# Attention: queries and keys projected and split once, spread into 64-row blocks by PE with 0/1 products, and the turned maxima added one step later

## The chip, the core and the metric

One core of a Trainium2 chip runs the whole program. The metric is the device time of one execution in microseconds (us). Five engines work side by side, each on its own list of instructions in order: PE (matrix products and 128x128 transposes, which end in PSUM), DVE (vector operations), ACT (element-wise functions), POOL (further element-wise operations and the indirect transfers) and SP (transfers). They are ordered against each other only by counting semaphores: an instruction can wait for a count, and everything behind it on its engine waits with it.

## What is computed

The reference runs a convolution-style block with sampled attention, then an ordinary attention layer, then a mixture of experts over four images of 256 tokens and 128 channels. The change is in the attention layer. Cut to what matters here (`_ln_t` is a layer norm over channels):

```python
q = heads(x @ wq.T)                       # 8 heads of 16 channels
k = heads(x @ wk.T)
v = heads(x @ wv.T)
attn = softmax(einsum('bhnd,bhmd->bhnm', q, k) * 16 ** -0.5)
out = einsum('bhnm,bhmd->bhnd', attn, v)
t = t + out @ wproj.T                     # with x = _ln_t(t)
...
t = t + ffn(_ln_t(t))                     # each token goes to 2 of 16 experts
```

## The kernel before

All of this is one program with its order written out by hand on every engine. After the sampled attention and a feed-forward layer (until 155 us of the profile) comes the attention, then the routing of tokens to experts, and the experts.

**Units and steps.** The attention is cut into 8 units (`UNITS`). Unit u is image b = u // 2 and one half of the heads, g = u % 2, so 4 heads (`UH`). All four engines go through `unit_step(k)` for k = 0 to 9, and in step k do a part of unit k+1 (make queries and keys), k (scores and their row maxima), k-1 (scores the other way round, exponentials) and k-2 (weighted values, division by the sum).

**64-row blocks.** To get products of fp32 accuracy out of the one-pass type fp32r, each query and key is split into a high part (the rounded value) and a low part (the rest). A head has 64 rows (`HROWS`) on the partition axis: for queries 16 rows of the high part, 16 of the low part, 16 of the high part again, and 16 rows for the negated row maximum and zeros; for keys high, high, low, and a row of ones (`one_row`, at row `SPLIT`). One product over the 64 rows then gives the whole score, less its maximum. Two heads lie above each other in 128 partitions.

**How the blocks come about before.** The weights `wq` and `wk` arrive from the host three times over (`thrice`, L1763), so that a projection lands in all of the rows. POOL splits these weights into `wqk_h` and `wqk_l` (L486 to L494). ACT writes the normed tokens twice, as `z1_h` (rounded, L716) and `z1` (L531), and DVE takes the difference `z1_l` (L1019). For each unit and for queries and keys apart, PE's `project(u, of_keys)` (L1460) runs 6 fp32r products of 256 columns into PSUM bank 6 or 7; ACT's `high_parts` (L653) writes the high parts, and DVE's `parts` (L1023) adds the low ones.

**The rest of a step.** `scores(u, pair)` (L1474) is 4 products for two heads; DVE's `row_max` (L1031) reduces each of the 4 heads; PE's `turn_max` (L1489) transposes the 4 maxima into bank 5, and DVE's `max_rows` (L1038) adds them to the queries. `scores_t(u, pair)` (L1500) then gives the transposed scores, ACT's `exp_scores` (L664) takes the exponentials, two at a time, `weigh_values` (L1513) multiplies them with the values, ACT's `unit_out` (L671) copies the result, PE's `turn_out` (L1528) transposes it, and DVE's `unit_norm` (L1045) divides by the sums.

**Waits around it.** PSUM banks 6 and 7 hold one projection each, so a new one waits for the last reader of the old one. Scores of unit k wait for its queries and keys (`qk_ready`), and `scores(k, 1)` for the maxima of `scores(k, 0)` (banks 0 and 1).

**After the loop.** In steps 8 and 9 (`k == UNITS` and the one behind it) the first half of the tokens goes on to its routing: `turn_outputs(0)`, `output_logits(0)`, `project_out(0)`, `rank(0)` on PE; `rank_logits(0)`, `choose(0)`, `residual(0)`, `moments`, `scale(0)` and `place(0)` on DVE. `place(0)` writes the slot numbers (`slots`, L1112), and POOL scatters the tokens with 16 indirect transfers (L514). The second half follows.

Of the kernel before, what the change touches and what calls it, by code (L numbers as in the profile page):

```python
# [55 lines left out]
def columns(**widths):  # L56

    at, where = 0, {}
    for name, n in widths.items():
# [7 lines left out]
                      geglu=2 * GE * P, denseT=GE * P, pout=C, wq=AH * HROWS, wk=AH * HROWS, wv=C, wproj=C, wprojT=C, gate=E)  # L67
# [5 lines left out]
def build(nc, x, weights, vectors, rows, w1_t, w2_t, out):  # L73
    with ExitStack() as ctx:
# [32 lines left out]
        row_groups = sb("row_groups", [P, 2, 4])  # L107
        row_group = sb("row_group", [P, 4])

        raw_by = sb("raw_by", [P, 2])  # L110
        high_by = sb("high_by", [P, 2])
        one_row = sb("one_row", [P, 1])
        sel = sb("sel", [P, 4, NP, P], BF16)
# [106 lines left out]
        with ExitStack() as rounded:  # L220
            xm, wqk_h, wqk_l, z1_h, z1_l = (rounded.enter_context(nc.sbuf_tensor(name, [P, n * T], F32R)) for name, n in (
                ("xm", 4), ("wqk_h", 1), ("wqk_l", 1), ("z1_h", 1), ("z1_l", 1)))
        late = sb("late", [P, 8 * T])
        xm_h, xm_l = (xm[:, 2 * n * T:2 * (n + 1) * T].rearrange("c (s t) -> c s t", s=2) for n in range(2))
# [69 lines left out]
        def sems(names):  # L294
# [27 lines left out]
        geglu_parted, hn_h_ready, hn_l_ready, wqk_parted, z1_h_ready, z1_l_ready = sems(  # L322
            "geglu_parted hn_h_ready hn_l_ready wqk_parted z1_h_ready z1_l_ready")
        gate_mm, lin_mm, gelu_ready, ff_ready, x1_mm, x1_ready = sems(
            "gate_mm lin_mm gelu_ready ff_ready x1_mm x1_ready")
        qk_mm, high_ready, qk_ready, v_mm, v_ready, zeroed = sems(
            "qk_mm high_ready qk_ready v_mm v_ready zeroed")
# [108 lines left out]
        def _(pool):  # L436
# [47 lines left out]
            wqk = w_sb[:, WAT["wq"][0]:WAT["wk"][1]]  # L484
            quarter = 2 * GE * P // 4
            for w, high, low, parted in ((W("geglu"), geglu_h, geglu_l, geglu_parted),  # L486
                                         (wqk, wqk_h[:, :], wqk_l[:, :], wqk_parted)):
                for n in range(4):
                    cols = slice(n * quarter, (n + 1) * quarter)
                    nc.gpsimd.tensor_tensor(high[:, cols], w[:, cols], one_c[:, 0:1].to_broadcast([P, quarter]),  # L490
                                            ALU.mult).then_inc(parted, 1)
                    pool.wait_ge(parted, 2 * n + 1)
                    nc.gpsimd.tensor_tensor(low[:, cols], w[:, cols], high[:, cols].bitcast(F32),
                                            ALU.subtract).then_inc(parted, 1)  # L494


# [22 lines left out]
        def _(act):  # L519
# [133 lines left out]
            def high_parts(u, of_keys):  # L653

                act.wait_ge(qk_mm, 2 * u + of_keys + 1)
                raw = ps[:, 6 + of_keys, :].rearrange("c (n t) -> c n t", n=2)
                if of_keys:
                    ins = nc.scalar.activation(of_unit(keys, u), raw, ACT.Identity, scale=high_by[:, 1:2],  # L658
                                               bias=one_row[:, 0:1])
                else:  # L660
                    ins = nc.scalar.activation(of_unit(queries, u), raw, ACT.Identity, scale=high_by[:, 0:1])  # L661
                ins.then_inc(high_ready, 1)
# [136 lines left out]
        def _(dve):  # L799
# [333 lines left out]
            def unit_step(k):  # L1133
# [17 lines left out]
                if k == 0:  # L1151
                    z1_rest(1)
# [642 lines left out]
```

## Time and profile before

| what | value |
|---|---|
| median of 3 runs | 278.84 us (278.82 to 282.73) |
| span of the profiled execution, first to last instruction | 279.1 us |
| busy: PE, DVE, ACT, POOL | 232.4, 207.5, 182.6, 48.9 us |
| attention steps 0 to 7, from the first scores to the last unit's scores | 158.86 to 202.36 us |
| slot numbers of the first tokens written | 217.02 us (start) |
| scatter by POOL, last transfer issued | 238.42 us |

The profile gives no time for the profiled execution other than its span; it stands 0.26 us (0.1%) above the median. A row of the timeline gives start, length, engine, source line, operation, output and inputs, and how many instructions are merged; a note in brackets says how long the engine had been idle, and what ended it. A row of the chain gives start, length and what the end of the program was waiting for at that time. An fp32 product shows as two instructions (x2), an fp32r product and a transpose as one.

### The profile page before, as it was taken

How to read it: one execution, taken by the hardware profiler on the slowest of the kernel's cores; microseconds unless marked ns; L12 is line 12 of the kernel's file. 1: busy time of each engine (PE TensorE's matmuls, PEld its weight loads, DVE VectorE, ACT ScalarE, POOL GpSimd, SP SyncE). 2: the span in 40 equal slices, each digit the busy share in tenths (PEclk: the TensorE clock that was granted, in tenths of full speed). 3: DMA queues.
4: the chain of work that ended last, by engine and by line, in shares of the span. 5: the costliest groups of instructions: out<-in, count | busy, mean ns of one | idle time of the engine just before them, and what ended most of it. 6: DMA issues, size and time to landing. Idle time of an engine off the chain costs nothing.

```text
span 279.1 us, 7576 instructions
## 1 busy us (share of the span) xinstructions
PE 232.4 (83%) x2920; PEld 161.5 (58%) x2920; DVE 207.5 (74%) x474; ACT 182.6 (65%) x274; POOL 48.9 (18%) x64
## 2 busy tenths in 40 slices
PE   0899469999999999949999957998888609999984
PEld 0589326767676767736897845666546603333361
DVE  4666896999999999965516778878868867857712
ACT  8768897989898989147615447676757395556500
POOL 7003918900000000010000200000000577200000
PEclk9999958999999999995999999999999656999999
DMA  6930000000000000293000000000000032396002
GB/s 155 348 130 4 0 0 2 0 2 0 0 0 0 0 0 0 92 383 131 0 0 4 0 0 2 0 2 0 4 0 4 29 105 83 118 384 263 2 2 75
DMA packets 9332, 16.22 MB, mean 58 GB/s; under 512 B 736, under 2 KB 6624, under 8 KB 9056
## 3 DMA queue, kind: packets, MB, share of 16 engines
q1 hardware_dynamic: 8800, 14.90, 15.3%
q0 software_dynamic: 512, 1.05, 1.2%
q8 instruction: 13, 0.21, 0.3%
q14 instruction: 7, 0.06, 0.1%
HBM read 12.80 MB, written 3.15 MB: 57 GB/s over the span
## 4 chain that ended last, share of the span: by engine, by line
PE 62%; DVE 12%; issue 7%; ACT 7%; POOL 5%; DMA 3%; SPq 1%; POOLq 0%; DVEq 0%; ACTq 0%
PE ps L1371 12%; PE ps L1355 9%; POOL slot_rows L514 5%; PE ps L1676 4%; ACT arena L600 4%; DVE t_k L1034 3%; PE ps L1470 3%; PE ps L1438 3%; PE ps L1523 3%; PE ps L1701 2%; PE ps L1484 2%; PE ps L1428 2%; PE ps L1425 2%; PE ps L1496 2%; DMA r_sb<-in_rows 2%
## 5 line engine op out<-in xcount | busy, mean ns | idle before, releaser
L600 ACT ACTIVATE arena<-ps,one_less_sq 128x1024 bf16<-128x1024 f32 x64 | 68.6, 1114 | 7.8 <-PE ps L1355 7.5
L1371 PEld LDWEIGHTS ps<-arena 128*128 128x128 bf16 x1536 | 47.7, 96 | 20.1 <-issue 8.0
L1371 PE MATMUL ps<-arena 128*128 (+1 forms) x1536 | 50.5, 184 | 2.2 <-ACT arena L600 2.1
L1355 PE MATMUL ps<-wide,sel 128*128 (+1 forms) x128 | 40.0, 397 | 7.8 <-ACT arena L600 5.9
L993 DVE TENSOR_REDUCE msda<-wide 128x768 f32 x32 | 45.2, 1454 | 0.0
L988 DVE TENSOR_TENSOR wide<-ps,wide 128x768 f32<-128x768 f32 x32 | 29.8, 951 | 4.5 <-PE ps L1371 4.5
L514 POOL DMA_INDIRECT slot_rows<-nrm,slots x16 | 16.8, 1051 | 65.4 <-DVE slots L1112 60.8
L1676 PE MATMUL ps<-arena,w_sb 128*32 x48 | 23.8, 629 | 0.3 <-ACT w_sb L779 0.3
L1034 DVE TENSOR_REDUCE t_k<-ps 128x2 f32<-128x512 f32 x32 | 20.5, 682 | 0.0
L669 ACT ACTIVATE wide<-ps 128x512 f32<-128x512 f32 x32 | 17.3, 594 | 1.4 <-PE ps L1508 1.3
L1684 PE MATMUL ps<-late,w_sb 128*32 128x512 f32 x80 | 17.9, 658 | 0.0
L1009 DVE SCALAR_TENSOR_TENSOR wide<-ps,v_sb,wide 128x512 f32<-128x512 f32 x8 | 6.0, 750 | 13.0 <-ACT wide L642 12.7
L1355 PEld LDWEIGHTS ps<-wide,sel 128*128 (+1 forms) x128 | 8.9, 97 | 11.5 <-ACT arena L600 7.3
L1027 DVE SCALAR_TENSOR_TENSOR xm<-ps,raw_by,xm 128x512 fp32r<-128x512 f32 x16 | 11.9, 747 | 3.7 <-ACT xm L658 1.9
L1190 DVE COPY late<-arena 128x512 f32 x34 | 12.0, 420 | 2.8 <-issue 2.8
L501 POOL MEMSET t_k<- 128x1024 f32 x1 | 1.0, 952 | 67.6 <-PE ps L1411 67.6
L1676 PEld LDWEIGHTS ps<-arena,w_sb 128*32 128x32 f32 x48 | 5.1, 115 | 13.2 <-issue 13.1
L539 ACT ACTIVATE sel<-minus_2j,sel_low,ident 128x128 bf16<-128x128 f32 x32 | 12.6, 480 | 0.0
L661 ACT ACTIVATE xm<-ps,high_by 128x512 fp32r<-128x512 f32 x8 | 5.5, 688 | 10.4 <-PE ps L1470 10.4
L790 ACT ACTIVATE sel<-ps 128x512 f32<-128x512 f32 x12 | 7.2, 598 | 7.5 <-PE ps L1684 7.5
L642 ACT ACTIVATE wide<-ps,v_sb 128x512 f32<-128x512 f32 x8 | 5.5, 688 | 8.8 <-PE ps L1428 8.8
L1659 PE MATMUL ps<-ident,late 128*128 128x128 f32 x24 | 4.7, 330 | 7.0 <-DMA late<-slot_rows 7.0
(315 smaller groups left out, 512.4 us busy)
## 6 DMA issues: line engine op xcount, KB each, us to landing
arena<-in_w_t SPq DMA_DIRECT2D x1, 4096.0 KB, 15.3
wide<-in_w_t SPq DMA_DIRECT2D x1, 4096.0 KB, 14.8
w_sb<-in_weights SPq DMA_DIRECT2D x1, 1544.0 KB, 8.9
late<-slot_rows SPq DMA_DIRECT2D x5, 256.0 KB, 3.3
slot_rows<-t_c SPq DMA_DIRECT2D x1, 896.0 KB, 11.3
slot_rows<-t_c SPq DMA_DIRECT2D x1, 640.0 KB, 9.6
x_sb<-in_x SPq DMA_DIRECT2D x4, 128.0 KB, 2.5
out<-xn SPq DMA_DIRECT2D x2, 256.0 KB, 2.2
```

The lines of the kernel that those rows point to most:

```text
L514: nc.gpsimd.indirect_dma_start(out=scratch[h], out_offset=bass.IndirectOffsetOnAxis(ap=slots[:, c, t:t + 1], axis=0), in_=nrm[:, t, :], in ...
L539: ins = nc.scalar.activation(sel[:, h, p, :], minus_2j[:, :], ACT.Identity, scale=ident[:, at:at + 1], bias=sel_low[:, h, p:p + 1])
L600: nc.scalar.activation(hot[:, u, 2 * c:2 * c + 2, :, :], ps[:, 2 * (c % 2):2 * (c % 2) + 2, :].rearrange("r p (b q) -> r p b q", b=B), ACT ...
L669: nc.scalar.activation(prob_t[u % 2][:, i, :], ps[:, 2 + i % 2, :], ACT.Exp).then_inc(prob_ready, 1)
L988: nc.vector.tensor_tensor(prod[:, c, :, :, :], g, w.unsqueeze(3).to_broadcast([P, 2, NP * NK, DH]), ALU.mult).then_inc(g_free, 1)
L993: nc.vector.tensor_reduce(msda[:, 4 * c + u:4 * c + u + 3:2, bass.ds(i, 1), :].rearrange("q b h d -> q b (h d)"), prod[:, c, :, :, :].rear ...
L1034: nc.vector.tensor_reduce(nmax[:, :, 2 * (u % 2) + i // 2, HROWS * (i % 2) + SPLIT], ps[:, i % 2, :].rearrange("q (t k) -> q t k", t=2), A ...
L1190: nc.vector.tensor_copy(staged_at[n % len(staged_at)], w1_sb[:, bass.ds(at[q][t - tiles_before(h, first)], 1), :].rearrange("d e f -> d (e ...
L1355: ins = nc.tensor.matmul(ps[:, 2 * (c % 2) + p % 2, :], sel[:, bass.ds(i % 4, 1), p, :].rearrange("k h j -> k (h j)"), terms_t[:, bass.ds( ...
L1371: ins = nc.tensor.matmul(ps[:, 4 + b, p * NK * DH:(p + 1) * NK * DH], hot[:, u, p, b, :], rhs, start=(s == 0), stop=(s == PARTS - 1))
L1676: nc.tensor.matmul(ps[0:GRAIN, 2 + t % 4, :], x_cols[:, t * P:t * P + GRAIN], w1_sb[:, bass.ds(at[j], 1), :].rearrange("d e f -> d (e f)"))
L1684: ins = nc.tensor.matmul(ps[GRAIN * q:GRAIN * (q + 1), 2 + t % 4, :], x_cols[:, t * P + GRAIN * q:t * P + GRAIN * (q + 1)], staged_at[entr ...
```

## The change

Queries and keys are projected once for each half of the tokens (two images), as plain fp32 products of 512 columns (`project(h, of_keys)`): 4 products in all. ACT copies the result rounded (`high_part`: `q_h`, `k_h`) and DVE takes the rest (`low_part`: `q_l`, `k_l`). For each unit PE then runs `spread(u, of_keys)`: 4 fp32r products of 256 columns over 64 rows, with matrices `spread_by` that hold the scale or 0, which copy the high and low parts to the rows of the 64-row blocks. ACT copies the blocks out (`queries_out`, `keys_out`). The tokens `z1` are written once. `wq` and `wk` come from the host once, not three times, which makes the last part of the weights' transfer 2320 columns in place of 3088. POOL makes `spread_by` where it had split `wq` and `wk`.

`turn_max` and `max_rows` of a unit go from the end of its own step into the next step; `weigh_values`, `unit_norm` and others have other places. Projections of the second half stand in steps 1 and 2, with `high_part` and `low_part`. In step 9 `rank(0)` and `input_logits(1)` stand ahead of the last unit's `weigh_values`.

```diff
+            nc.gpsimd.tensor_tensor(of_64[:, :, :, :].rearrange("r n j d -> r (n j d)"), ident[:, 0:HROWS], ident[:, HROWS:P],
+                                    ALU.add).then_inc(pool_step, 1)
...
-            def high_parts(u, of_keys):
...
+            def high_part(h, of_keys):
+
+                act.wait_ge(qk_mm, 2 * h + of_keys + 1)
+                nc.scalar.activation(half(k_h if of_keys else q_h, h), ps[:, 6 + of_keys, :], ACT.Copy).then_inc(high_ready, 1)
+
+            def queries_out(u):
+
+                act.wait_ge(spread_mm, 2 * u + 1)
+                nc.scalar.activation(of_unit(queries, u), ps[:, 6, :].rearrange("c (n t) -> c n t", n=2),
+                                     ACT.Copy).then_inc(qk_ready, 1)
+
+            def keys_out(u):
+
+                act.wait_ge(spread_mm, 2 * u + 2)
+                nc.scalar.activation(of_unit(keys, u), ps[:, 7, :].rearrange("c (n t) -> c n t", n=2), ACT.Identity,
+                                     bias=one_row[:, 0:1]).then_inc(qk_ready, 1)
...
             def unit_step(k):
+                if k in (1, 2):
+                    high_part(1, k - 1)
                 if k + 1 < UNITS:
-                    high_parts(k + 1, 0)
-                if k >= 2:
-                    unit_out(k - 2)
+                    queries_out(k + 1)
                 if k >= 1 and k - 1 < UNITS:
                     exp_scores(k - 1, 0)
                     exp_scores(k - 1, 1)
+                if k >= 2:
+                    unit_out(k - 2)
+                if k == 0:
+                    ln_out(lns["lna"], 4, z1, halves=(1,))
                 if k + 1 < UNITS:
-                    high_parts(k + 1, 1)
+                    keys_out(k + 1)
...
-            def parts(u, of_keys):
...
+            def low_part(h, of_keys):
+
+                dve.wait_ge(high_ready, 2 * h + of_keys + 1)
+                high, low = (k_h, k_l) if of_keys else (q_h, q_l)
+                nc.vector.tensor_tensor(half(low, h), ps[:, 6 + of_keys, :], half(high, h).bitcast(F32),
+                                        ALU.subtract).then_inc(low_ready, 1)
...
                 if k < UNITS:
                     row_max(k, 0)
                     row_max(k, 1)
-                if k + 1 < UNITS:
-                    parts(k + 1, 0)
-                if k >= 2:
-                    unit_norm(k - 2)
+                if k in (1, 2):
+                    low_part(1, k - 1)
+                if k >= 1 and k - 1 < UNITS:
+                    max_rows(k - 1)
...
-            z1_rest(0)
+            low_part(0, 0)
+            low_part(0, 1)
             dve.wait_ge(x1_mm, 8)
             ln_stats(lns["lna"], summed(2), 1)
-            dve.wait_ge(dve_consts, 2)
-            parts(0, 0)
-            parts(0, 1)
             input_deviation(0)
...
+            def project(h, of_keys):
+
+                pe.wait_ge(lns["lna"]["out"], h + 1)
+                if h:
+
+                    pe.wait_ge(qk_ready, 2 * of_keys + 3 + of_keys)
+                nc.tensor.matmul(ps[:, 6 + of_keys, :], W("wk" if of_keys else "wq"), half(z1, h)).then_inc(qk_mm, 1)
+
+            def spread(u, of_keys):
 
                 b, g = u // 2, u % 2
+                h = b // 2
+                pe.wait_ge(low_ready, (2 if u > of_keys + 1 else 0) + of_keys + 1)
                 if u:
 
-                    pe.wait_ge(qk_ready, 2 * u - 1 + of_keys)
...
+                    pe.wait_ge(qk_ready, 2 * (u - 1) + of_keys + 1)
+                high, low = (k_h, k_l) if of_keys else (q_h, q_l)
+                rows = slice(HROWS * g, HROWS * g + HROWS)
+                for n in range(2):
+                    for s, part in enumerate((high, low)):
+                        ins = nc.tensor.matmul(ps[:, 6 + of_keys, n * HW:(n + 1) * HW], spread_by[rows, of_keys, s, n, :],
+                                               part[rows, b * HW:(b + 1) * HW], start=(s == 0), stop=(s == 1))
+                ins.then_inc(spread_mm, 1)
```

Three places show the new order. The first is PE in one step of the steady run, from `scores(k, 0)` on. In the names, `ps` is PSUM, `xm` the queries and keys, `t_k` the maxima, `wide` the exponentials and values, `proj` the weighted values. Before:

```order
L1484 MATMUL ps<-xm 128x256 [waits nmax_ready,qk_ready]
L1484 MATMUL ps<-xm 128x256 x3
L1470 MATMUL ps<-z_h,wqk_h 128x256 [waits z1_l_ready,qk_ready]
L1470 MATMUL ps<-z_h,wqk_l 128x256
L1470 MATMUL ps<-z_l,wqk_h 128x256
L1470 MATMUL ps<-z_h,wqk_h 128x256
L1470 MATMUL ps<-z_h,wqk_l 128x256
L1470 MATMUL ps<-z_l,wqk_h 128x256
L1523 MATMUL ps<-wide 32x256 [waits o_raw_ready,prob_ready,v_ready]
L1523 MATMUL ps<-wide 32x256 x7
L1508 MATMUL ps<-xm 128x256 [waits prob_ready,nmax_t_ready]
L1508 MATMUL ps<-xm 128x256 x3
```

In the changed kernel the same stretch of PE, from `scores(k, 0)` (L1491) on, reads:

```order
L1491 MATMUL ps<-xm 128x256 x3
L1503 MATMUL ps<-ident,t_k 128x128 [waits o_ready,nmax_ready]
L1503 MATMUL ps<-ident,t_k 128x128 x3
L1477 MATMUL ps<-q_h,spread_by 128x256 [waits qk_ready,low_ready]
L1477 MATMUL ps<-q_l,spread_by 128x256
L1477 MATMUL ps<-q_h,spread_by 128x256
L1477 MATMUL ps<-q_l,spread_by 128x256
L1491 MATMUL ps<-xm 128x256 [waits nmax_ready,qk_ready]
L1491 MATMUL ps<-xm 128x256 x3
L1515 MATMUL ps<-xm 128x256 [waits prob_ready,nmax_t_ready]
L1515 MATMUL ps<-xm 128x256 x3
L1530 MATMUL ps<-wide 32x256 [waits o_raw_ready,prob_ready,v_ready]
```

Six products of the projection have become four of the spread; the turn of the maxima (L1503) comes right behind the first scores, and the second scores (L1491) come ahead of the transposed scores (L1515) and of the weighted values (L1530).

The second place is ACT ahead of step 0: before, it writes the tokens twice (`z_h`, `q_c`), then the first queries and keys (`xm`).

```order
L716 ACTIVATE z_h<-ps 128x512 [waits lna_turned]
L531 ACTIVATE q_c<-ps 128x512 [waits lna_turned]
L661 ACTIVATE xm<-ps,high_by 128x512 [waits qk_mm,dve_consts]
L658 ACTIVATE xm<-ps,one_row,high_by 128x512 [waits qk_mm]
L524 ACTIVATE ln_std<-ln_mv,eps_c 128x4 [waits lna_var]
```

In the changed kernel the same place of ACT reads:

```order
L540 ACTIVATE q_c<-ps 128x512 [waits lna_turned]
L665 ACTIVATE q_h<-ps 128x512 [waits qk_mm,dve_consts]
L665 ACTIVATE k_h<-ps 128x512 [waits qk_mm]
L533 ACTIVATE ln_std<-ln_mv,eps_c 128x4 [waits lna_var]
L670 ACTIVATE xm<-ps 128x512 [waits spread_mm]
L676 ACTIVATE xm<-ps,one_row 128x512 [waits spread_mm]
```

The first queries and keys (`xm`) now stand behind the standard deviation of the second half (`ln_std`), which stood behind them before.

The third place is PE in step 9, the end of the attention (`pair_sq` and `ceil_b` belong to `rank(0)`, `q_c` to `input_logits(1)`). Before:

```order
L1523 MATMUL ps<-wide 32x256 [waits o_raw_ready,prob_ready,v_ready]
L1523 MATMUL ps<-wide 32x256 x7
L1538 MATMUL ps<-ident,proj 128x128 [waits o_ready,nmax_t_ready,o_raw_ready]
L1538 MATMUL ps<-ident,proj 128x128
L1591 MATMUL ps<-ceil_b,ones_b 128x16 [waits chosen_ready]
```

In the changed kernel the same step on PE reads:

```order
L1598 MATMUL ps<-ceil_b,ones_b 128x16 [waits chosen_ready]
L1599 MATMUL ps<-pair_sq,tok_before 128x48
L1602 MATMUL ps<-pair_sq,ones_b 128x48
L1602 MATMUL ps<-pair_sq,ones_b 128x32
L1602 MATMUL ps<-pair_sq,ones_b 128x16
L1571 MATMUL ps<-w_sb,q_c 128x16 x4
L1530 MATMUL ps<-wide 32x256 [waits o_raw_ready,prob_ready,v_ready]
L1530 MATMUL ps<-wide 32x256 x7
L1545 MATMUL ps<-ident,proj 128x128 [waits o_ready,nmax_t_ready,o_raw_ready]
L1545 MATMUL ps<-ident,proj 128x128
```

The weighted values of the last unit (L1530) and their turn (L1545) now stand behind the ranks and the logits of the second half.

## Rows read from the trace of the kernel before

**Rows 1.** The page: the span of the profiled execution.

```profile
span 279.1 us, 7576 instructions
```

**Rows 2.** Chain that ended last: start us, length us, what; attention to scatter.

```profile
178.68 0.50 PE ps L1484 x4
...
202.36 0.50 PE ps L1484 x4
...
214.84 0.29 DVE msda L1053
...
217.02 0.27 DVE slots L1112
...
238.42 2.36 DMA slot_rows<-nrm,slots
...
245.39 0.41 PE ps L1676
```

**Rows 3.** Timeline of one steady step: start us, us, engine line op out<-in xcount [idle before].

```profile
190.52 0.51 PE L1484 MATMUL ps<-xm 64*128 64x256 f32 x4
190.56 0.69 DVE L1042 TENSOR_TENSOR xm<-xm,ps 128x512 fp32r<-128x512 f32 x1
...
190.96 0.38 PE L1470 MATMUL ps<-z_h,wqk_h 128*128 128x256 f32 x1
...
191.16 1.28 DVE L1034 TENSOR_REDUCE t_k<-ps 128x2 f32<-128x512 f32 x2
...
191.29 0.28 PE L1470 MATMUL ps<-z_l,wqk_h 128*128 128x256 f32 x1
191.30 0.19 PEld L1470 LDWEIGHTS ps<-z_h,wqk_h 128*128 128x128 f32 x1
191.41 0.28 PE L1470 MATMUL ps<-z_h,wqk_h 128*128 128x256 f32 x1
...
191.86 1.07 PE L1523 MATMUL ps<-wide 128*32 128x256 f32 x16
191.96 0.69 ACT L661 ACTIVATE xm<-ps,high_by 128x512 fp32r<-128x512 f32 x1 [1.42 <-PE ps L1470]
...
192.86 0.50 PE L1508 MATMUL ps<-xm 64*128 64x256 f32 x4
192.99 0.39 ACT L676 ACTIVATE proj<-ps 128x256 f32<-128x256 f32 x1 [0.34 <-PE ps L1523]
...
193.39 1.09 ACT L669 ACTIVATE wide<-ps 128x512 f32<-128x512 f32 x2
...
193.53 0.44 PE L1538 MATMUL ps<-ident,proj 128*128 128x128 f32 x2
...
194.00 0.21 DVE L1051 RECIPROCAL inv_sum<-ps 128x8 f32<-128x8 f32 x1 [0.56 <-PE ps L1538]
```

**Rows 4.** Timeline ahead of step 0, and the exponentials' table in step 1.

```profile
152.69 0.60 ACT L716 ACTIVATE z_h<-ps 128x512 fp32r<-128x512 f32 x1 [2.03 <-PE ps L1256]
...
155.37 0.89 DVE L811 BATCH_NORM_STATS2 ln_st<-ps 128x6 f32<-128x128 f32 x4 [0.87 <-PE ps L1438]
...
156.30 0.38 DVE L814 BATCH_NORM_AGGREGATE ln_mv<-ln_st 128x2 f32<-128x6 f32 x4
...
157.47 0.29 ACT L524 ACTIVATE ln_std<-ln_mv,eps_c 128x4 f32<-128x4 f32 x1
...
158.86 0.50 PE L1484 MATMUL ps<-xm 64*128 64x256 f32 x4 [0.41 <-DVE lg L1069]
...
168.86 1.28 ACT L669 ACT_TABLE_LOAD   x1
```

**Rows 5.** Timeline of step 9: the logits of the second half on PE.

```profile
214.32 1.04 PE L1564 MATMUL ps<-w_sb,q_c 128*128 128x16 f32 x8
```

**Rows 6.** Windows: from:to, us, busy of PE PEld DVE ACT POOL, PEclk, DMA, GB/s.

```profile
160.00:165.00 5.00, 2.07 (x17) 1.56 (x15) 4.09 (x7) 2.79 (x5) 0.00 (x0) 1.00 0.00 0
220.00:225.00 5.00, 3.12 (x19) 2.33 (x17) 4.66 (x26) 2.26 (x6) 3.78 (x5) 0.50 0.15 46
```

More of the change, by code:

```diff
@@ L711, in unit_step @@
                     nc.scalar.activation(table_junk[:, :], eps_c[:, :], ACT.Sqrt)
-            def z1_out(h):
-                act.wait_ge(lns["lna"]["turned"], 4 * (h + 1))
-                nc.scalar.activation(half(z1_h, h), ps[:, 4 + h, :], ACT.Identity).then_inc(z1_h_ready, 1)
-                ln_out(lns["lna"], 4, z1, halves=(h,))
             ln_std_of(lns["lna"], (0,))
-            z1_out(0)
+            ln_out(lns["lna"], 4, z1, halves=(0,))
             act.wait_ge(dve_consts, 2)
-            high_parts(0, 0)
-            high_parts(0, 1)
+            high_part(0, 0)
+            high_part(0, 1)
             ln_std_of(lns["lna"], (1,))
+            queries_out(0)
+            keys_out(0)
             values_out(0)
@@ L1603, in unit_step @@
                     scores(k, 0)
-                if k + 1 < UNITS:
-                    project(k + 1, 0)
-                if k >= 2:
-                    weigh_values(k - 2)
-                if k >= 1 and k - 1 < UNITS:
-                    scores_t(k - 1, 0)
+                if k >= 1 and k - 1 < UNITS:
+                    if k == 1:
+                        pe.wait_ge(x1_ready, 2)
+                    turn_max(k - 1)
+                if k == 0:
+                    turn(lns["lna"], 4, (1,))
+                if k in (1, 2):
+                    project(1, k - 1)
+                if k + 1 < UNITS:
+                    spread(k + 1, 0)
                 if k < UNITS:
                     scores(k, 1)
-                if k >= 2:
-                    turn_out(k - 2)
+                if k == 0:
+                    values_of(1)
                 if k == UNITS:
@@ L1618, in unit_step @@
                     input_logits(1)
-                if k == 0:
-                    turn(lns["lna"], 4, (1,))
+                if k >= 1 and k - 1 < UNITS:
+                    scores_t(k - 1, 0)
+                if k >= 2:
+                    weigh_values(k - 2)
                 if k + 1 < UNITS:
-                    project(k + 1, 1)
-                if k == 0:
-                    values_of(1)
+                    spread(k + 1, 1)
                 if k >= 1 and k - 1 < UNITS:
                     scores_t(k - 1, 1)
+                if k >= 2:
+                    turn_out(k - 2)
                 if k == UNITS - 1:
@@ L1642, in _ @@
             input_logits(0)
+            pe.wait_ge(spread_by_ready, 8)
+            pe.wait_ge(dve_consts, 2)
+            spread(0, 0)
+            spread(0, 1)
             for k in range(UNITS + 2):
```

106 lines of the change are left out of this document (35 added, 71 removed).

## The prediction

> **What bounds the kernel now.** The profiled execution spans 279.1 us [rows 1]. I read the chain of waits from its end backwards first. The last 41 us hang on POOL's scatter: the slot numbers start at 217.02, the last scatter lands from 238.42 on, and 16 indirect transfers stand between, one behind the other [rows 2]. So whatever happens in the attention counts through one moment only: when the slot numbers of the first tokens are written. It passes to the end in full, because the second half's slots hang on the same DVE list behind it. The reader is to see in the same chain that the steady steps are 178.68 to 202.36 for four units, 5.92 us each [rows 2], and that 14.9 us follow from the last unit's first scores to the end of the slots (202.36 to 217.29).
>
> Then the timeline of one step [rows 3] shows what a step hangs on. No engine is full: PE waits, and DVE holds the loop together. The scores start at 190.52, the projection at 190.96, the weighted values at 191.86, ACT copies them at 192.99, PE turns the copy at 193.53, DVE divides at 194.00 and only then reduces the second pair of heads, whose maxima PE turns before the next scores. The change takes this loop apart: the division is no longer ahead of the second maxima.
>
> **What is removed and added, engine by engine.** Per unit, DVE loses two `parts` and keeps all else. PE runs 8 products of the spread in place of 12, 0.12 each (191.29 to 191.41 [rows 3]): 0.5 less. Against that stand four fp32 projections of 512 columns: an fp32 product has two passes of 0.43 (0.41 of it in the chain at 245.39 [rows 2]), so 0.86 each, 3.4 in all, against 8 x 0.5 = 4.0 saved. In sum PE gains almost nothing; what counts is the order. ACT's copies: 0.60 without an operand (152.69 [rows 4]), 0.69 with one (191.96 [rows 3]); so `queries_out` 0.60 and `keys_out` 0.69. The smaller weight transfer and POOL's work lie more than 90 us ahead of the attention; I count them at nothing, covered by the sampled attention; if that cover were gone, PE would be seen waiting for POOL ahead of the first spread.
>
> **The steady step, worked out.** Time 0 is the start of `scores(k, 0)`. Prices from [rows 3]: a group of 4 products 0.44 until the next group; the maxima of a pair start 0.64 behind the scores and take 1.28; `max_rows` 0.69; exponentials start 0.53 behind their scores, 1.09 a pair; weighted values 1.0 (191.86 to 192.86). The result of a group of six reaches ACT 1.00 after its start (190.96 to 191.96), so of four 2 x 0.12 sooner, 0.76. 0.05 passes at each handing over.
> - first maxima 0.64 to 1.92; meanwhile PE turns the old maxima and spreads (until 1.32)
> - `scores(k, 1)` 1.97; `max_rows(k-1)` 1.9 to 2.55
> - `scores_t(k-1, 0)` 2.60; weighted values 3.04 to 4.04
> - spread of the keys 4.04, at ACT 4.80; `keys_out` until 5.49 (ACT is free from 4.6: exponentials 3.13 to 4.22, `unit_out` 0.39)
> - next `scores` 5.54.
>
> The other ends come earlier: the second maxima end at 3.9, `turn_out` at 5.1. I take 5.5: 0.42 less than 5.92, over the four steady steps 178.68 to 202.36 **-1.7 us**.
>
> A rule of the Trainium skill speaks against this price. The trace first: in the projection the load of the next weights (0.19) starts at 191.30 while the product of 191.29 runs, and the next product starts 0.12 later [rows 3], with all loads on the same 128 rows. "TensorE: Matmul & The Clock Gate" (Part 3, row/col tiling) states that a weight load overlaps with products in flight only when their row groups differ; the four products of a spread all sit on the same 64 rows. By the row a spread costs 0.44, by the rule 4 x (0.12 + 0.19) = 1.2 at most, and the sum would be some 6 us longer. This case's trace does not bear the rule out for 128 rows; a run of 64-row products on one row group is not in it. I take the row.
>
> **The lead-in and steps 0 to 2.** Here the change makes the way longer. PE is free for the projection at about 155.2 either way (the statistics that wait for the same products start at 155.37 [rows 4]). Queries projected until 156.1, seen by ACT at 156.3, `high_part` to 156.9, `low_part` to 157.6; keys one after: `low_part` to 158.4. Meanwhile PE runs values and logits, about 0.9 each (1.04 for such a group in [rows 5]), until 158.8 and spreads until 159.7. The statistics of the second half, at 155.37 before, now stand on DVE behind both `low_part`: 158.3 to 159.6 (0.89 and 0.38 [rows 4]), the deviation on ACT 159.9 (0.29), and only behind it `queries_out` 160.5 and `keys_out` 161.2. First scores 161.2, not 158.86: **+2.3**.
>
> Step 0 gets shorter (one copy of z1, not two, no difference): maxima, three copies on ACT, `queries_out(1)`, z1 and values, spread, `keys_out(1)`: 161.2 to 166.4. Steps 1 and 2 hold a new wait. The spread for unit 2 waits for `low_part` of the projection that stands right ahead of it, since both use bank 6; behind it on PE wait `scores(1, 1)`, `scores_t(0, 0)` and all that follows. Step 1: projection 167.3 to 168.2, `high_part` to 168.9, `low_part` to 169.6, spread, `queries_out(2)` to 170.8, the exponentials' table 1.28 [rows 4], a pair of exponentials, `keys_out(2)` to 174.0: 7.6 long. Step 2: here the keys' spread stands late in the step, but `low_part` holds `max_rows(1)` on DVE until 177.9, and with it the transposed scores, the weighted values, the spread and `keys_out(3)`: 180.9. Before, the same scores started at 178.68: **+2.2** so far, the lead-in included.
>
> **The tail.** From the start of `scores(7, 0)` = 0, by the same prices: `scores_t(6, 0)` 2.6, weighted values (5) 3.0 to 4.0, `unit_out` 4.6, `turn_out(5)` 4.75; `unit_norm(5)` 5.2 to 5.7 (0.47 behind the turn, 193.53 to 194.00 [rows 3]). Only then may the maxima of unit 7 be turned (same bank): 5.8, added until 7.1, where before this stood in step 7 itself. `output_logits(0)` runs 6.5 to 7.4, transposed scores 7.4, weighted values (6) to 8.8, `turn_out(6)` 9.5, `project_out(0)` 9.8 to 10.7. Then `rank(0)` 0.2 and `input_logits(1)` 0.85 ahead of the last weighted values: 11.75 to 12.75; copy 13.3, turn 13.35, division 13.8 to 14.3, and `scale(0)` and `place(0)` behind it on DVE. Before, that division stood at 214.84 = 12.5, ended 12.8, and the slots ended 2.16 later at 14.9 [rows 2]; DVE's own work ahead of it started no earlier. Now 14.3 + 2.1 = 16.4: **+1.4** (16.4 less 14.9, rounded down, since my sums by rounded steps run a little long).
>
> **Sum.** +2.2 - 1.7 + 1.4 = +1.9 against the profiled span of 279.1 [rows 1]; that span stands 0.26 above the median, so I add the difference to the median: 278.84 + 1.9 = **280.7 us**. Bounds of the prices: a spread between 0.34 (two groups 0.34 apart, were pairs to overlap: about -0.1 on each spread, -0.2 x 8 and a little more = -1.5) and 1.2 at worst, with every load of 0.19 bare (0.8 more, on the path in eight places from the lead-in to the last keys = +6); a projection pass between 0.22 (if it were one pass of 0.43 for a product, -0.43 in three places on the path = -1.3) and 0.5 (+0.5).
>
> **Rivals.**
> - *The spread's weight loads don't hide.* If half to two thirds of each load of 0.19 [rows 3] stands bare, a spread takes 0.8 to 0.9 and puts 0.4 on each path through `keys_out`; the steady step is 5.9 again and nothing is given back: 282 to 284. For it: all four products use the same 64 rows; against it: the load at 191.30, which did hide. (It is the rule named above that would bring this about.) Shown by steps of 5.9 and a spread over 0.6.
> - *The other side: TensorE's clock falls in steps 1 and 2* and the kernel is clearly slower. The granted clock was 0.50 (1.2 of 2.4 GHz) at 220 to 225, after PE had stood in the waits of the routing [rows 6]. In steps 1 and 2 PE now works about 3.7 of 7. At half the clock its share of some 3 us on the path doubles in both steps: +6, so 286 to 287; it decides from about one and a half such steps on. Against it: at 160 to 165 PE was busy 2.07 of 5 and kept 1.00 [rows 6].
> - *The lead-in and the tail cost less than I sum*, by waits that already lay there: if half of +2.2 and +1.4 is absorbed, 278.9; with the cheap end of the spread or the projection 277.
> - *The change doesn't shorten the steps and doesn't lengthen the ends*: about 278.8, within the forecast's range.
> - *Faster by over 2%* would need 5.6 us less; with the ends as worked out each of the four steps would have to be 1.9 shorter than mine, 3.6, and PE alone has 4.3 in a step (nine groups: six of 0.44, 0.44 for the turn, 1.0 and 0.22).
>
> **How the numbers follow.** 2% (5.6 us) is about what a measurement of this kernel can tell from no change. Forecast as worked out, 279.0 to 282.0: 0.55. Loads that don't hide, 282.0 to 284.4: 0.17. Cheaper ends, 276 to 279: 0.18. Clock or another loss over 284.4: 0.08. Under 273.3: 0.02. The range 277.6 to 283.6 leaves about 2 in 10 outside. Within 2%: 0.55 + 0.17 + 0.18 = 0.90.
>
> **What would show it.** In the changed profile: first scores at about 161 and a DVE that does the second statistics at 158; steps of 7.6 and 6.9 and then of 5.5; in steps 1 and 2 a PE gap of over 1 us ahead of a spread, ended by DVE's `low_part`; the last weighted values behind `input_logits`, the slots at about 219 and the scatter as long as before. Wrong would be: a spread far from 0.44, steady steps of 5.9 or under 5.2, a clock under 1.00 before 215, or a scatter that no longer follows the slots.

## The result and the profile after

The changed kernel takes **287.36 us** (median of 4 runs, 286.61 to 288.12) against 278.92 for the one before: the ratio of the runs is **1.0239, 95% interval 1.0186 to 1.0291**. (The two medians alone give 1.030; one of the four executions of before took 282.73.) So the change costs 6.7 us by the ratio, 7.0 by the profiled spans and 8.4 by the medians. Medians and ratios, here and below, leave out executions that took over 1.5% longer than the fastest of the same kernel. The forecast was 280.7 with a range up to 283.6; the time lies beyond it, just above the place of the rival "TensorE's clock falls in steps 1 and 2", 286 to 287. The page of the profiled execution, its span and the granted clock (in tenths of 2.4 GHz) in 40 slices of 7.15 us:

```profile
span 286.1 us, 7514 instructions
PEclk9999959999999999978999755599999855999999
```

The same line before, in slices of 6.98 us:

```profile
PEclk9999958999999999995999999999999656999999
```

Slices 22 to 25, counted from 0 (157 to 186 us), are the news: 7 and 5 in place of 9. The other low slices (5; 17 and 18; 31 to 33) have their like before, in the sampled attention and in the routing [rows 6].

Where the time went, by the start of `scores(k, 0)` in the timeline of PE:

```profile
159.66 0.50 PE L1491 MATMUL ps<-xm 64*128 64x256 f32 x4 [1.18 <-ACT xm L676]
...
166.60 0.80 PE L1491 MATMUL ps<-xm 64*128 64x256 f32 x4 [0.78 <-ACT xm L676]
...
176.52 0.72 PE L1491 MATMUL ps<-xm 64*128 64x256 f32 x4
...
186.49 0.51 PE L1491 MATMUL ps<-xm 64*128 64x256 f32 x4 [0.18 <-ACT xm L676]
...
191.92 0.51 PE L1491 MATMUL ps<-xm 64*128 64x256 f32 x4 [0.17 <-ACT xm L676]
...
208.18 0.51 PE L1491 MATMUL ps<-xm 64*128 64x256 f32 x4 [0.17 <-ACT xm L676]
```

Steps 0, 1 and 2 take 6.94, 9.92 and 9.97; forecast were 5.2, 7.6 and 6.9. The steady steps take 5.42 ((208.18 - 186.49) / 4), forecast 5.5, before 5.92. The slots of the first tokens are written here:

```profile
224.45 0.25 DVE L1114 TENSOR_REDUCE slots<-picked_slot 128x6 int32<-128x96 f32 x1
```

That is 16.5 behind `scores(7, 0)` (forecast 16.4, before 14.9 [rows 2]). So the steady steps and the tail came out as worked out, and the whole miss lies between 160 and 186 us. There the windows of one microsecond (busy us of PE, PEld, DVE, ACT, POOL, each with its count; granted clock; DMA share, GB/s) show:

```profile
157.00:158.00 1.00, 1.00 (x10) 0.97 (x10) 0.96 (x7) 0.00 (x0) 0.00 (x0) 1.00 0.00 0
158.00:159.00 1.00, 0.48 (x5) 0.27 (x3) 0.71 (x7) 0.75 (x3) 0.00 (x0) 1.00 0.00 0
159.00:160.00 1.00, 0.34 (x4) 0.30 (x4) 1.00 (x4) 1.00 (x4) 0.00 (x0) 1.00 0.00 0
160.00:161.00 1.00, 1.00 (x10) 0.74 (x7) 0.89 (x3) 1.00 (x3) 0.00 (x0) 1.00 0.00 0
161.00:162.00 1.00, 0.71 (x6) 0.53 (x6) 0.56 (x1) 0.62 (x3) 0.00 (x0) 0.79 0.00 0
162.00:163.00 1.00, 0.92 (x6) 0.62 (x6) 0.49 (x1) 0.54 (x2) 0.00 (x0) 0.50 0.00 0
```

The clock goes from 2.4 to 1.2 GHz at about 161.6 and stays there until about 185.5, some 24 us. What PE did ahead of the fall and just behind it (start, length, line, rows x columns of the weights, output):

```profile
153.77 1.88 PE L1463 MATMUL ps<-q_c,w_sb 128*128 128x512 f32 x4
...
157.49 0.28 PE L1477 MATMUL ps<-q_l,spread_by 64*128 64x256 f32 x1
157.61 0.28 PE L1477 MATMUL ps<-q_h,spread_by 64*128 64x256 f32 x1
...
160.10 0.66 PE L1253 MATMUL ps<-ident,nrm 128*128 128x128 f32 x4
...
161.71 0.80 PE L1491 MATMUL ps<-xm 64*128 64x256 f32 x4 [0.29 <-DVE t_k L1036]
...
162.59 2.08 PE L1554 MATMUL ps<-w_sb,q_c 128*128 128x128 f32 x8
...
168.23 1.92 PE L1463 MATMUL ps<-q_c,w_sb 128*128 128x512 f32 x2
```

PE stood still for 1.18 and 0.29 us. Before, it stood 0.41 ahead of the first scores [rows 4], and then twice for longer, as two rows of its timeline show that have not been shown yet:

```profile
161.54 0.50 PE L1484 MATMUL ps<-xm 64*128 64x256 f32 x4 [1.28 <-DVE t_k L1034]
...
165.19 1.16 PE L1547 MATMUL ps<-w_sb,q_c 128*128 128x128 f32 x8 [1.84 <-ACT q_c L531]
```

and the window 160 to 165, with PE busy for 2.07 of 5, kept 1.00 [rows 6]. In the 7.8 us from the first projection on PE was busy for 6.47 in the changed kernel, and the clock fell; before, for 6.12, and it held. So the fall can't be told by idleness alone. What does differ: from 157.3 on nearly all of PE's products use **64 rows** of the array (the spreads and the scores), where before the projections in between used 128. From 162 on PE's prices go up, most of them to nearly double: the values 2.08 (1.16 at full clock, in the row of before above), a projection 0.86 per pass in place of 0.43, four scores 0.80 in place of 0.50.

### The profile page after: what moved, and what is told of

Its sections match the earlier page's. It is cut to its first block, busy times and chain, and to the rows that moved or that the text cites. A ratio compares the mean times of both kernels' runs of the same rounds, so it can differ in the third digit from the quotient of the medians.

```text
span 286.1 us, 7514 instructions
## 1 busy us (share of the span) xinstructions
PE 238.7 (83%) x2896; PEld 163.1 (57%) x2896; DVE 197.7 (69%) x456; ACT 181.9 (64%) x276; POOL 47.8 (17%) x66
## 4 chain that ended last, share of the span: by engine, by line
PE 63%; ACT 9%; issue 8%; DVE 8%; POOL 5%; DMA 3%; SPq 1%; POOLq 0%; DVEq 0%; ACTq 0%
PE ps L1368 12%; PE ps L1352 9%; POOL slot_rows L523 5%; PE ps L1686 4%; ACT arena L609 3%; PE ps L1435 3%; PE ps L1491 3%; PE ps L1530 2%; PE ps L1711 2%; PE ps L1477 2%; PE ps L1515 2%; PE ps L1463 2%; DVE t_k L1036 2%; ACT xm L676 2%; DMA r_sb<-in_rows 2%
## 5 line engine op out<-in xcount | busy, mean ns | idle before, releaser
L1352 PE MATMUL ps<-wide,sel 128*128 (+1 forms) x128 | 39.2, 390 | 8.2 <-ACT arena L609 6.4
L1491 PE MATMUL ps<-xm 64*128 64x256 f32 x64 | 10.7, 373 | 4.5 <-ACT xm L676 2.8
L1515 PE MATMUL ps<-xm 64*128 64x256 f32 x64 | 10.6, 352 | 2.4 <-ACT wide L684 2.0
L1491 PEld LDWEIGHTS ps<-xm 64*128 64x128 f32 x64 | 7.0, 223 | 7.3 <-ACT xm L676 4.5
## 6 DMA issues: line engine op xcount, KB each, us to landing
arena<-in_w_t SPq DMA_DIRECT2D x1, 4096.0 KB, 14.9
```

The source lines that it names most:

```text
L1352: ins = nc.tensor.matmul(ps[:, 2 * (c % 2) + p % 2, :], sel[:, bass.ds(i % 4, 1), p, :].rearrange("k h j -> k (h j)"), terms_t[:, bass.ds( ...
L1491: ins = nc.tensor.matmul(ps[:, i % 2, t * HW:(t + 1) * HW], of_head(queries, u, i)[:, t * P:(t + 1) * P], of_head(keys, u, i))
L1515: ins = nc.tensor.matmul(ps[:, 2 + i % 2, t * HW:(t + 1) * HW], of_head(keys, u, i)[:, t * P:(t + 1) * P], of_head(queries, u, i))
```

## The experiments

Three theories stood against each other: the clock falls because PE is *idle* too long; it falls because its products use few *rows*; or the loss is one of *structure* (the waits for `low_part`), and the clock only goes with it. The expectations call the last the structure theory, and speak of a clock theory where either of the first two will do. All starts below are read from the timelines of one profiled execution each; "slots written" is the end of the slots, and the last column gives the length of each stretch at half clock. The stretch ahead of the attention varies by some 2 us from one execution to the next, so the moment of the fall is given from the start of the first projection (153.77 in the changed kernel; the fall is 7.8 behind it).

| kernel | projection | scores of unit 0 | 1 | 2 | 3 | 7 | slots written | fall, behind the projection | half clock, 155 to 212 |
|---|---|---|---|---|---|---|---|---|---|
| before | 155.09 | 158.86 | 166.72 | 172.75 | 178.67 | 202.36 | 217.3 | none | 0 |
| changed | 153.77 | 159.66 | 166.60 | 176.52 | 186.49 | 208.18 | 224.7 | 7.8 | 24 |
| gap filled, 128 rows | 153.96 | 159.87 | 165.40 | 174.54 | 182.97 | 204.66 | 222.2 | 11.8 | 3.4, 6.8, 3.4 |
| gap filled, 64 rows | 155.62 | 161.52 | 168.46 | 178.38 | 186.71 | 208.39 | 224.9 | 8.8 | 17 |
| all waits filled | 153.47 | 159.38 | 165.46 | 173.22 | 180.12 | 201.81 | 218.3 | none | 0 |
| projections in other banks | 153.69 | 159.59 | 167.68 | 175.68 | 183.00 | 204.68 | 221.2 | 7.8 | 20 |
| spread on 128 rows | 153.78 | 159.67 | 164.82 | 172.58 | 180.98 | 202.69 | 219.2 | 18.6 | 3.4 |
| old order in the tail | 155.44 | 161.34 | 168.27 | 178.19 | 186.45 | 208.14 | 223.8 | 8.7 | 17 |
| before, 64 rows | 154.57 | 158.56 | 167.97 | 175.06 | 183.09 | 206.79 | 221.7 | 8.5 | 6.8, 6.8 |
| all together, 128-row spread | 154.69 | 160.59 | 164.99 | 170.03 | 175.57 | 197.27 | 213.0 | none | 0 |

**Filling the first gap, with 128 and with 64 rows.** One gap, the same number of idle products (nine, read by nobody), and only their rows differ:

```
             spread(0, 1)
+            for _ in range(9):     # rows: 0 to 127, or 0 to 63
+                nc.tensor.matmul(ps[:, 5, 0:HW], spread_by[rows, 0, 0, 0, :], q_h[rows, 0:HW])
             for k in range(UNITS + 2):
```

> The changed kernel with nine idle products put into PE's gap of 1.18 us between the last spread of unit 0 and the first scores (158.4 to 159.66): operands of 128 rows x 128 columns against 256, into bank 5, which is free there; nothing reads them. Idle theory (the clock falls because PE stands still too long in the lead-in and steps 0 to 2): the granted clock falls later than 161.8, or not at all; each half-clock microsecond that goes away gives about 0.3 back, so 283 to 287. Row theory (the clock falls because from 157.3 on nearly all products use only 64 rows): the same fall is put off here, since the fillers use 128 rows. Structure theory (the loss of 7 us comes from the waits for low_part and the order, the clock is only seen beside it): wherever the clock falls, scores of unit 3 stay within 0.5 of 186.5 and the time at 286 to 288.

> As the run with 128 rows, but the nine idle products use rows 0 to 63 alone (64 x 128 against 256), so that PE is busy for the same time. Idle theory: the clock behaves as with 128 rows. Row theory: the clock falls at 161.8 as without fillers, within 0.5 us, and the time stays at 286 to 288.

Measured, one run each: 285.14 and 287.59 us. First the run with 128 rows, where values and spread keep their full-clock price and the fall comes at 165.8:

```profile
158.61 1.33 PE L1610 MATMUL ps<-q_h,spread_by 128*128 128x256 f32 x9
...
162.80 1.16 PE L1554 MATMUL ps<-w_sb,q_c 128*128 128x128 f32 x8 [0.38 <-ACT q_c L540]
...
166.75 1.91 PE L1463 MATMUL ps<-q_c,w_sb 128*128 128x512 f32 x2
```

And the run with 64 rows, where the values are slow already:

```profile
160.19 1.24 PE L1610 MATMUL ps<-q_h,spread_by 64*128 64x256 f32 x9
...
164.46 2.08 PE L1554 MATMUL ps<-w_sb,q_c 128*128 128x128 f32 x8 [0.38 <-ACT q_c L540]
```

Both gaps are filled for nearly the same time. With 64 rows the clock falls 8.8 behind the projection. That is later than in the changed kernel (7.8) by more than the half microsecond expected, but the run with the old tail, which has no filler at all and is the changed kernel up to step 9, fell 8.7 behind it: no effect of the 64-row fillers can be seen. With 128 rows the fall is put off to 11.8. Over the first 8.8 us from the projection PE was busy alike, for 8.17 with 128 rows, where the clock held, and for 8.08 with 64, where it fell. That is against the idle theory, which wanted both alike, and against the structure theory, since the scores of unit 3 stood at 182.97 in the one run and not near 186.5; but it is one execution of each.

**Filling the waits of steps 0 to 2** with products of 128 rows (9 in the lead-in, then 10, 12, 10 and 8) tells what the change costs without its clock:

```
                 if k in (1, 2):
                     project(1, k - 1)
+                    if k == 1:
+                        pe.wait_ge(v_ready, 2)
+                        fill(12, 4)
```

> The changed kernel with idle products of 128 rows in the gap of the lead-in (9) and in the four waits of steps 0 to 2: behind the last spread of step 0 (10), behind the projection (12) and behind the last spread (10) of step 1, behind the second scores of step 2 (8). Clock theory: the granted clock stays at 1.00 from 150 to 215, the scores of unit 3 start at 180 to 181 in place of 186.5, all behind them moves by as much, and the time is 281 (280 to 282.5). Structure theory: the scores of unit 3 stay at 186 and the time at 286 to 288, whatever the clock.

Measured: 282.11 us, ratio 1.0067 (1.0042 to 1.0092). The clock held:

```profile
155.00:210.00 55.00, 50.50 (x430) 36.02 (x432) 34.56 (x75) 33.34 (x63) 0.59 (x1) 1.00 0.00 1
```

and the scores of unit 3 came within the expected 180 to 181:

```profile
173.22 0.50 PE L1491 MATMUL ps<-xm 64*128 64x256 f32 x4
...
180.12 0.50 PE L1491 MATMUL ps<-xm 64*128 64x256 f32 x4 [0.17 <-ACT xm L676]
```

Steps 1 and 2 took 7.76 and 6.90; the prediction has 7.6 and 6.9. Step 0 took 6.08, where the prediction has 5.2. Of its runs' own before (279.9) the ratio is +1.9 us (1.2 to 2.6), and +1.9 is the sum of the prediction. From unit 0's to unit 3's scores the changed kernel needs 26.83, this one 20.74: **the clock costs 6.1 us** in the profiled execution of the changed kernel. It is not always as much: the run with the old tail, the same kernel up to step 9, had 17 us of half clock in place of 24 and needs 25.11, which makes it 4.4; the two ratios (1.0239 and 1.0067) put it at 4.8. The rival had put it at 6.

**The spread on 128 rows.** The sharpest test adds no product and moves none: the 0/1 matrix gets zeros in the rows of the other unit.

```
-                        ins = nc.tensor.matmul(..., spread_by[rows, of_keys, s, n, :],
-                                               part[rows, b * HW:(b + 1) * HW], ...)
+                        ins = nc.tensor.matmul(..., spread_by[:, g, of_keys, s, n, :],
+                                               part[:, b * HW:(b + 1) * HW], ...)
```

> The changed kernel, but each product of the spread uses all 128 rows: the 0/1 matrix has zeros in the rows of the other unit, so that the sum, the number of products, their columns and PE's order are the same, and only the rows in use are doubled (POOL builds the larger matrix in 16 parts of 64 partitions, far ahead). Row theory: the clock, which fell at 161.8 in the changed kernel, is held through 164 at least and falls later or not at all; the time is 281 to 285. Idle theory (only how long PE stands still counts): the clock falls at 161.8 within 0.5 of the same place in the program as before this edit, and the time is 286 to 288.

Measured: 282.64 us, ratio 1.0106 (1.0043 to 1.0169). PE is now idle as long as in the changed kernel ahead of the first scores (1.27 here, 1.18 there) and ahead of the spread in step 1 (1.41 in both), and yet the values and the projection of the queries run at their full-clock price; the clock falls only at 172.4, at the end of step 1 and behind a stand of 1.84, and is back at 175.8:

```profile
159.67 0.51 PE L1494 MATMUL ps<-xm 64*128 64x256 f32 x4 [1.27 <-ACT xm L679]
...
162.41 1.16 PE L1557 MATMUL ps<-w_sb,q_c 128*128 128x128 f32 x8 [0.19 <-ACT q_c L543]
...
165.75 1.02 PE L1466 MATMUL ps<-q_c,w_sb 128*128 128x512 f32 x2
...
168.18 0.38 PE L1480 MATMUL ps<-q_h,spread_by 128*128 128x256 f32 x1 [1.41 <-DVE q_l L1033]
```

The idle theory wanted the fall at 161.8 and 286 to 288. Half clock went from 24 us to 3.4 by rows alone. The 3.4 is that of the profiled execution, the one of four with the highest mean clock over its span, 0.939; the other three have 0.933, 0.927 and 0.921, which by an estimate from these means is 3 to 10 us more of half clock, somewhere in the program. All four executions of the changed kernel lie lower, at 0.904 or 0.905. Step 0 took 5.15 (forecast 5.2), step 1 7.76, step 2, with the rest of the half clock in it, 8.40. Products of 128 rows follow each other as closely as those of 64, by 0.12 us in both.

**The same in the kernel before, the other way round.** The projections of units 0 to 3 multiply rows 0 to 63 only and leave out half of each sum:

```
+                        rows = slice(0, HROWS if u <= 3 else P)
                         ins = nc.tensor.matmul(ps[:, 6 + of_keys, j * HW:(j + 1) * HW],
-                                               w[:, at_w:at_w + P], z[:, b * HW:(b + 1) * HW], ...)
+                                               w[rows, at_w:at_w + P], z[rows, b * HW:(b + 1) * HW], ...)
```

> The kernel before, but the projections of units 0 to 3 (those in the lead-in and steps 0 to 2) multiply only rows 0 to 63 of the weights and of the input: half of each sum is left out, while the number of products, their 256 columns, their order and every wait stay. Row theory: the clock, which stayed at 1.00 from 155 to 215, falls here as well, somewhere between 159 and 170, and the scores of unit 3 come 1.5 to 6 later than 178.7; the time is 281 to 285. Idle theory: nothing changes, since PE stands exactly as long as before (1.00 throughout, 279 to 280).

Measured: 285.33 us, ratio 1.0164 (1.0098 to 1.023). Nothing but the rows of four units' projections differs, and the clock falls at 163.0, at a place that before passed at 1.00:

```profile
162.96 0.32 PE L1471 MATMUL ps<-z_l,wqk_h 64*128 64x256 f32 x1
165.11 2.08 PE L1548 MATMUL ps<-w_sb,q_c 128*128 128x128 f32 x8 [1.84 <-ACT q_c L531]
```

The stand of 1.84 is the one of before, to the hundredth. The scores of unit 3 come 4.4 later than in before (183.09 against 178.67). Both executions have a mean clock of 0.909; the seventeen of before beside them lie at 0.921 to 0.939. This shows from the other side that rows alone bring the clock down.

**Taking the waits out, clock left alone.** Queries of the second half projected into bank 5 at the end of step 0, keys into bank 4 at the end of step 1:

```
-                if k in (1, 2):
-                    project(1, k - 1)
...
                     spread(k + 1, 1)
+                if k in (0, 1):
+                    project(1, k)       # banks 5 and 4 in place of 6 and 7
```

> The changed kernel with the second half's projections taken out of the spread's banks: queries projected into bank 5 at the end of step 0, keys into bank 4 at the end of step 1, parted at the end of the same steps, so that no spread waits for low_part of the projection right ahead of it. Structure theory: steps 1 and 2 lose the waits (7.6 and 6.9 by the prediction become about 6 and 5.5), some 5 us less whatever the clock: 281 to 283. Clock theory: the clock decides; if the 0.86 of a 128-row projection in step 0 holds it at 1.00, the scores of unit 3 start at 177.5 to 179 and the time is 278 to 280; if it falls all the same, 283 to 286.

Measured: 284.28 us, ratio 1.0142 (1.0086 to 1.0197): the clock fell all the same, 7.8 behind the projection and so ahead of the moved work, and the time is that expected for this case. No spread waits for `low_part` any more, and steps 1 and 2 still take 8.00 and 7.32. From unit 0's to unit 3's scores it is 23.41 in place of 26.83: the waits, and the somewhat shorter half clock (20 us in place of 24), are worth 3.4 us together, not the 5 that the structure theory wanted. This run also shows PE busy without a break and still at half clock:

```profile
170.00:175.00 5.00, 5.00 (x20) 3.13 (x18) 2.28 (x4) 3.49 (x5) 0.00 (x0) 0.50 0.01 3
175.00:180.00 5.00, 5.00 (x33) 3.81 (x36) 3.72 (x6) 3.15 (x7) 0.00 (x0) 0.50 0.00 0
```

So no stand of PE keeps the clock down there.

**The order in the tail, put back.**

```
-                if k == UNITS + 1:
-                    rank(0)
-                    input_logits(1)
...
                     turn_out(k - 2)
+                if k == UNITS + 1:
+                    rank(0)
+                    input_logits(1)
```

> The changed kernel with one order put back: in the last step of PE's list the weighted values of unit 7 and the turn behind them stand ahead of rank(0) and input_logits(1), not behind. Theory of the tail (+1.4 to +1.6 of the slots' end are this order and the turned maxima in step 8): the way from scores(7, 0) to the slots' end falls from 16.5 to 15.4, the time by 1.1 (0.8 to 1.4). Rival (DVE is held by its own list there, choose and residual): the way stays within 0.3 of 16.5.

Measured: 286.13 us, ratio 1.0212 (1.0142 to 1.0283), which can't be told from the 1.0239 of the changed kernel; so only the profile decides. The last weighted values start at 218.97 here, 10.83 behind `scores(7, 0)`; in the changed kernel at 220.02, 11.84 behind. First the changed kernel:

```profile
219.04 1.04 PE L1571 MATMUL ps<-w_sb,q_c 128*128 128x16 f32 x8
220.02 1.07 PE L1530 MATMUL ps<-wide 128*32 128x256 f32 x16
```

And with the old order:

```profile
217.99 1.06 PE L1584 MATMUL ps<-w_sb,xn 128*128 128x128 f32 x8
218.97 1.07 PE L1530 MATMUL ps<-wide 128*32 128x256 f32 x16
220.72 0.44 PE L1545 MATMUL ps<-ident,proj 128*128 128x128 f32 x2 [0.67 <-ACT proj L691]
```

To the end of the slots it is 15.7, not 16.5: 0.8 of the tail's 1.6 is this order, at the low edge of what was expected. That the other half comes from the turned maxima in step 8 is not shown; it was not tried by itself.

**Everything together.** The runs point to a version without the half clock and without the waits: both projections of the second half in bank 4 in step 1, the keys of unit 1 spread right behind its queries, the exponentials' table loaded in step 0, the old order in the tail; once with nine idle products in the first gap, once with the spread on 128 rows and no idle product. Beside them the kernel before with only the early table:

```
                     ln_out(lns["lna"], 4, z1, halves=(1,))
+                    nc.scalar.activation(table_junk[:, :], eps_c[:, :], ACT.Exp)
```

> The changed kernel with what the runs so far point to, together: the nine idle products of 128 rows ahead of the first scores; the second half's projections in bank 4 (queries and keys both in step 1, so that no spread waits for them); the keys of unit 1 spread right behind its queries and copied ahead of the second half of z1; the exponentials' table loaded in step 0, where ACT waits; the weighted values of unit 7 ahead of rank(0). Clock theory together with the working by steps: the clock stays at 1.00 from 150 to 215, steps 0, 1 and 2 are about 4.7, 5.1 and 5.7 (changed kernel with the clock held by fillers: 6.1, 7.8 and 6.9), the scores of unit 3 start at 175 to 176.5, and the time is 275.5 (274 to 278), against 279 to 280 of before. If the clock falls all the same: 279 to 283.

> The version with everything (second half's projections in bank 4, keys of unit 1 early, table loaded in step 0, tail order) but without idle products: the spread uses 128 rows with zeros in the other half's. Row theory: the clock stays at 1.00 from 150 to 210 without a single idle product, steps 0 to 2 take 4.6, 5.0 and 5.6, and the time is 276 (275 to 277.5), 1 to 1.5 per cent under before. Idle theory: the clock falls at about 161.8 and the time is 279 to 283.

> The kernel before with one addition: the exponentials' table (1.28 at 168.86) is loaded in step 0 by an idle exponential behind the second half of z1, where ACT waits. It shows how much of the version with everything any kernel could have. Expected: the first exponentials 1.1 to 1.3 earlier, the scores of unit 2 as much, and the time 1.0 (0.5 to 1.3) less than before; if step 1 hangs on the keys' projection instead, no change.

Measured: with idle products 276.13 us, ratio 0.9877 (0.9816 to 0.9939); with the 128-row spread **275.39 us, ratio 0.9805 (0.9765 to 0.9845)**; before with the early table 279.81, ratio 0.9970 (0.9943 to 0.9998). In the 128-row version the steps are 4.40, 5.04 and 5.54, and the clock is whole, though PE stands 1.28 ahead of the first scores:

```profile
160.59 0.51 PE L1498 MATMUL ps<-xm 64*128 64x256 f32 x4 [1.28 <-ACT xm L680]
...
170.03 0.45 PE L1498 MATMUL ps<-xm 64*128 64x256 f32 x4
...
175.57 0.51 PE L1498 MATMUL ps<-xm 64*128 64x256 f32 x4
```

```profile
155.00:210.00 55.00, 48.64 (x423) 32.87 (x422) 37.73 (x95) 37.55 (x71) 1.81 (x3) 1.00 0.01 1
```

The table alone gives 0.8 in before (step 1 takes 5.22 in place of 6.03), less than its 1.28: behind the first exponentials ACT now waits 0.49 for the keys' projection. The rest of the 5.5 us that the 128-row version gains comes from all its other edits together; which of them before could have had too was not tried.

## Why the prediction was wrong, step by step

- **The bound** held: the slots moved by 7.4 (217.3 to 224.7), and the span by 7.0. Counted from the first projection, which started 1.3 later in the profiled execution of before (155.09 against 153.77), the slots moved by 8.7. That is the sum of the four parts: +2.1 in the lead-in, +7.0 in steps 0 to 2, -2.0 in the steady steps, +1.6 in the tail.
- **The lead-in** (+2.3) was right: from the projection to the first scores 3.8 before, 5.9 after, +2.1. That the absolute 161.2 came out as 159.66 is the earlier start.
- **Steps 1 and 2** (7.6 and 6.9) were right at full clock, as the run with all waits filled shows: 7.76 and 6.90. Step 0 (5.2) took 6.08 there, with idle products in it, and 5.15 with the spread on 128 rows, without any. The wait of the spread for `low_part` is there as forecast (1.41 idle ahead of it, ended by DVE).
- **The steady step** (5.5) was 5.42. The price of the spread, 0.44, was right: the last spread and the four scores behind it take 0.90 together (206.67 to 207.57). The products on the same 64 rows follow each other by 0.12 (157.49, 157.61 above), so the rule of the Trainium skill on weight loads and row groups ("TensorE: Matmul & The Clock Gate", Part 3), weighed in the prediction, is not borne out here either.
- **The tail** (+1.4) was +1.6. So with the clock held the sum of +1.9 is what was measured by the ratio; in the profile of that run the slots come 2.7 later, counted from the projection, and the long step 0 is about the difference.
- **The step that failed** is that the sum takes every price of PE at full clock, and with it the dismissal of the rival: "Against it: at 160 to 165 PE was busy 2.07 of 5 and kept 1.00 [rows 6]". The row is true, but it was read for how long PE was busy, not for what it was busy with. The 17 products in that window hold projections of 128 rows, which the change takes out; the 64-row run of before is at half clock from 163.0 on in the same window. The chance of 0.08 was too small. The price of the rival (+6, so 286 to 287) came out near the 6.1 partly by luck: it had +3 in each of steps 1 and 2, and against the run with all waits filled it was 0.9 in step 0, 2.2 in step 1 and 3.1 in step 2. The fall came a step earlier than the rival put it, 2 us into step 0, and behind no stand of PE longer than 1.2.

The Trainium skill ("TensorE: Matmul & The Clock Gate", Part 1) states that the gate follows how busy PE is and closes when PE has been idle. Read as time in work, this would treat the two runs with a filled gap alike (PE busy for 8.17 and 8.08 us), and would drop the clock in before sooner than in the changed kernel (6.12 against 6.47). The traces go the other way in both; the measurement decides.

What stays open: why the clock falls where it does within those microseconds, how the rows are weighed, and what brings the clock back. The steady steps hold 1.00 although six of their nine groups use 64 rows; there PE is busy for 20.29 of 21.69 us. But the run with other banks, as busy and with whole projections of 128 rows in between, stayed at half clock for 20 us: the rows show in the fall, and no run here tells what they do to its end. The two runs with one gap filled are one execution each; what carries the row theory are the spread on 128 rows and the kernel before on 64.

## What to carry to other kernels

When a change swaps products, compare not only their number and columns but the rows that they use, above all where PE also waits: here half the rows cost 4 to 6 us through the clock, in stretches that showed no long idle time. Where a product of few rows can be given zeros for the rest of the array at no price, that is a cure that adds no product; it is not shown to be better than idle products (ratios 1.0106 against 1.0067 in the changed kernel, 0.9805 against 0.9877 in the version with everything, with intervals that overlap). And where new work waits for the work right ahead of it because both use one bank (the spread behind the projection), another bank for one of them takes the wait out.

## What was not expected of the hardware

- Whether the granted clock falls depends here on the rows in use: with the same order of products, the same columns and no product more, the changed kernel was at 1.2 GHz for 24 us with a spread of 64 rows, and for 3.4 us with one of 128 (each in its profiled execution), although half of those 128 rows multiplied by zeros; the kernel before went from 0 to 13.6 us when four units' projections lost half of their rows.
- Rows cost no time at full clock: a spread of 64 and one of 128 rows both start a product each 0.12 us.
- Work alone did not bring the clock back: with other banks PE was busy for 10 of 10 us from 170 to 180, at 1.2 GHz.
- Half the clock didn't double the steps: 24 us of it cost 6.1 and 17 us cost 4.4, about a quarter; PE is on the path for only part of a step.
